# A GRU recurrence whose gate inputs are written to PSUM by ScalarE instead of matmuls

## The chip, the cores and the metric

The kernel runs on one core of a Trainium2 chip. Five engines work beside each other, each through its own instructions in order: TensorE (PE in the profile, its weight loads PEld), VectorE (DVE), ScalarE (ACT), GpSimd (POOL) and SyncE (SP), which here only issues DMA transfers. They wait for each other through semaphores. The metric is device time of one execution in microseconds (us), as the median of several runs; lower is better.

## What is computed

The reference adds four layers' outputs to x, of shape (4, 512, 512). The change lies in the third, a GRU over the 512 time steps of each of the 4 batch rows, with a state of 512:

```python
def cell(h, x):
    gi = x @ W_ih + b_ih
    gh = h @ W_hh + b_hh
    i_r, i_z, i_n = jnp.split(gi, 3, axis=-1)
    h_r, h_z, h_n = jnp.split(gh, 3, axis=-1)
    r = jax.nn.sigmoid(i_r + h_r)
    z = jax.nn.sigmoid(i_z + h_z)
    n = jnp.tanh(i_n + r * h_n)
    h_new = (1.0 - z) * n + z * h
    return (h_new, h_new)
xs = jnp.swapaxes(inputs, 0, 1)
_, hs = jax.lax.scan(cell, initial_state, xs)
...
x = x + _L0_cond_ref(...)          # top-k over masked attention
x = x + _L1_cond_ref(...)          # attention, 16 heads
x = x + _L2_cond_ref(cond_2048, x, L2_cond_W_ih, L2_cond_W_hh, L2_cond_b_ih, L2_cond_b_hh)   # the GRU
x = x + _L3_cond_ref(...)          # transformer block, called DiT below
```

The input products gi of all steps are made before the loop. What is left for the loop is h @ W_hh and the gates, one step after the other.

## The kernel before, in words

`program` runs the layers one after another: the top-k layer, the small attention, `gate_input_phase` (it computes gi of all 512 steps), `gru_phase` (the recurrence), `dit_phase`. Between two phases all engines meet at a barrier. The change lies in `gru_phase`.

**Layout.** A column vector of 512 lies as KD = 4 chunks of 128 partitions, with B = 4 batch columns each. Chunks 0 and 1 are the half called a (`first`), chunks 2 and 3 the half called b (`second`). W_hh is split in two fp16 parts, `w_hh_hi` and `w_hh_lo`; so is the state (`state_parts`). The product needs weights hi by both state parts (`high`, 8 moving columns) and weights lo by the high part of the state (`low`, 4 columns). A gate's half needs 2 output chunks by 4 contraction chunks. One `low` or `high` call is 4 matmuls, each with its own weight load; a step calls them 24 times, 96 matmuls in all. There are four PSUM banks for the r and z gates of the two halves (`sum_ra`, `sum_rb`, `sum_za`, `sum_zb`), of 16 columns in use each, and four for the n gate (`sum_n`: two parities of the step by two halves).

**Where gi enters.** For r and z, gi of all steps lies in the SBUF buffer `room` as two fp16 parts (`gi_rz`). SyncE copies it, two steps at a time, into `gi_now` (two buffers), and four matmuls per step (`bring`, L1494) multiply it with a scaled identity and so open the four gate banks with it. For n, ScalarE copies `gi_n` of the next step into a slot of the n bank (`copy_gi_n`, L1590); TensorE waits for it on the semaphore `gn_ready`.

**One step.** TensorE: four `bring` matmuls, each behind a wait for VectorE's reading of that bank; the wait for `hi_a`, the new high part of the state's half a; 12 calls up to the last one for ra (`ra_sum`); 8 more, which end za, na, rb and zb (`rb_sum`, `zb_sum`); 4 calls for the half b of n. VectorE sums a gate bank's two parts (`total`, L1650), scans (`chain`, L1654) for r * h_n + gi_n and for the new state, and makes the low part of the state. ScalarE makes the sigmoids and tanhs. The new half a of the state comes out as: `ra_sum`, total of ra, sigmoid (L1601), scan for n (L1654), tanh (L1607), scan for the state (L1654, `hi_a`). Half b follows the same way, up to `hi_b` and `lo_b`, which TensorE waits for later in the next step.

**Order.** It is written out by hand for every engine. ScalarE's in a step is r, z and keep of half a (L1601, L1603, L1604), `copy_gi_n` for the next step (L1590), tanh of a (L1607), r, z and keep of half b (L1609, L1611, L1612), tanh of b (L1614), and a copy of the new state to the history (L1617). TensorE loops over four steps, ScalarE and VectorE over two.

**After the loop.** SyncE loads the DiT layer's first weights into `region[1]` and `region[0]`, the two halves of `room`, once the last `gi_now` has been loaded from there; TensorE turns the history back, VectorE adds it to X, and SyncE stores three quarters of X to DRAM (`x_gru`). The phase ends when these stores have landed.

## Time and profile before

| | us |
|---|---|
| median of 3 runs | 4073.15 |
| lowest and highest | 4071.14, 4074.32 |
| span of the profiled execution | 4078.2 |
| first gate-input matmul of step 0 | 1079.5 |
| first gate-input matmul of step 511 | 2494.6 |

The profile is of one execution of its own, whose span, from the first to the last instruction, is 5.05 us (0.12%) over the median of the timed runs; no other time of that execution is given. Times in its rows are counted from the start of the span. Start and duration of an instruction stand in front of its engine and line; a row for several matmuls in a row has their count behind (x4) and their time from the first one's start to the last one's end. The end of a matmul is modelled, its start is recorded. Instructions on one engine overlap in part, so the start of one to the start of the next is what counts, not the duration.

### The profile page before, as it was taken

To read this page: it belongs to the slowest core of one execution; us is meant where nothing else is said; L and a number is where in the kernel's file an instruction comes from. 1 tells how busy PE (TensorE), PEld (TensorE's weight loads), DVE (VectorE), ACT (ScalarE), POOL (GpSimd) and SP (SyncE) were. 2 spreads that over 40 slices of the span, in tenths; PEclk is the share of its full clock that TensorE was granted. 3 is DMA by queue.
4 is the path that set the end of the run, shared out by engine and by line. 5 is a ranking of instruction groups with operands and counts; after the bars stand their busy time and mean duration, and the time that the engine had idled before them with its cause. 6 is when DMAs were issued, how large, how long until landed. Compare 5 with 4: busy or idle time off the path is not lost. (4 is left out here: it accounts for less than half of the span.)

```text
span 4078.2 us, 177223 instructions
## 1 busy us (share of the span) xinstructions
PE 3719.3 (91%) x70140; PEld 2792.5 (68%) x70140; DVE 2749.4 (67%) x10621; ACT 2082.2 (51%) x7371; POOL 478.1 (12%) x411
## 2 busy tenths in 40 slices
PE   2458888888999999999999998999999999999999
PEld 2425465554699999999999996565456546644664
DVE  8878788786677777777777776576367537653763
ACT  4028678677755555555555553453245315532542
POOL 2006366364000000000000000001000100010001
PEclk9979999998755555555555556999999999999999
DMA  2023132231000000000000003211221141023102
GB/s 93 1 89 94 48 110 87 60 106 56 4 6 6 6 6 6 6 6 6 6 6 6 6 6 137 83 41 42 109 90 34 42 158 52 23 83 124 44 14 93
DMA packets 113888, 203.31 MB, mean 50 GB/s; under 512 B 44076, under 2 KB 76844, under 8 KB 111416
## 3 DMA queue, kind: packets, MB, share of 16 engines
q1 hardware_dynamic: 113720, 201.00, 14.8%
q8 instruction: 114, 1.87, 0.2%
q14 instruction: 54, 0.44, 0.0%
HBM read 160.05 MB, written 32.52 MB: 47 GB/s over the span
## 5 line engine op out<-in xcount | busy, mean ns | idle before, releaser
L1521 PE MATMUL gru_sum_n<-gru_state_parts,w_hh_hi 128*128 128x8 f16 x8192 | 499.6, 174 | 0.0
L1511 PE MATMUL gru_sum_n<-gru_state_parts,w_hh_lo 128*128 128x4 f16 x8192 | 488.9, 168 | 0.0
L1511 PEld LDWEIGHTS gru_sum_n<-gru_state_parts,w_hh_lo 128*128 128x128 f16 x8192 | 376.5, 104 | 0.0
L1521 PEld LDWEIGHTS gru_sum_n<-gru_state_parts,w_hh_hi 128*128 128x128 f16 x8192 | 376.5, 104 | 0.0
L653 ACT ACTIVATE dit_prob<-dit_bank,dit_head_nbias 128x512 f32<-128x512 f32 x256 | 175.9, 687 | 351.0 <-DVE dit_head_nbias L671 350.6
L1654 DVE TENSOR_TENSOR_SCAN gru_n_in<-gru_reset_gate,gru_sum_n 128x32 f32<-128x32 f32 x1024 | 225.4, 220 | 54.7
L1511 PE MATMUL gru_sum_rb<-gru_state_parts,w_hh_lo 128*128 128x4 f16 x4096 | 261.3, 168 | 0.0
L1521 PE MATMUL gru_sum_za<-gru_state_parts,w_hh_hi 128*128 128x8 f16 x4096 | 254.1, 169 | 0.0
L1521 PE MATMUL gru_sum_ra<-gru_state_parts,w_hh_hi 128*128 128x8 f16 x4096 | 254.1, 168 | 0.0
L1521 PE MATMUL gru_sum_zb<-gru_state_parts,w_hh_hi 128*128 128x8 f16 x4096 | 254.1, 168 | 0.0
L1511 PE MATMUL gru_sum_zb<-gru_state_parts,w_hh_lo 128*128 128x4 f16 x4096 | 252.1, 166 | 0.0
L1511 PE MATMUL gru_sum_ra<-gru_state_parts,w_hh_lo 128*128 128x4 f16 x4096 | 252.1, 166 | 0.0
L1511 PE MATMUL gru_sum_za<-gru_state_parts,w_hh_lo 128*128 128x4 f16 x4096 | 252.1, 166 | 0.0
L1650 DVE TENSOR_REDUCE gru_r_in<-gru_sum_ra 128x8 f32<-128x16 f32 x512 | 89.2, 174 | 240.9 <-PE gru_sum_ra L1521 240.9
L1601 ACT ACTIVATE gru_reset_gate<-gru_r_in 128x8 f32<-128x8 f32 x512 | 111.1, 217 | 272.9 <-DVE gru_r_in L1650 272.9
L1654 DVE TENSOR_TENSOR_SCAN gru_state_parts<-gru_keep_gate,gru_new_and_old 128x24 f16<-128x24 f32 x1024 | 212.3, 207 | 45.8
L1617 ACT ACTIVATE gru_hist<-gru_state 128x16 f32 x512 | 118.7, 232 | 238.1 <-DVE gru_state L1654 238.1
L1844 POOL TENSOR_TENSOR dit_gated_bias<-dit_gates,dit_bias_rows 128x1024 f32<-128x1024 f32 x4 | 9.4, 2345 | 1835.8 <-DVE dit_bias_rows L2129 1559.8
L635 PE MATMUL small_bank<-ident,small_prob 128*128 128x128 f32 x1024 | 165.9, 285 | 56.6 <-DVE small_turned L762 39.4
L1762 PE MATMUL dit_bank<-dit_qk 128*128 128x512 f16 x768 | 207.6, 379 | 1.3 <-DVE dit_qk L2142 1.3
L539 PE MATMUL dit_bank<-room,dit_V 128*128 128x512 f16 x512 | 195.6, 382 | 10.3 <-DVE dit_V L2210 10.3
L756 ACT ACTIVATE small_prob<-small_bank,small_head_nmax 128x512 f32<-128x512 f32 x256 | 176.2, 690 | 54.3 <-DVE small_head_nmax L665 49.9
(335 smaller groups left out, 12378.5 us busy)
## 6 DMA issues: line engine op xcount, KB each, us to landing
dit_w_qk<-w_qk_parts SPq DMA_DIRECT2D x64, 512.0 KB, 3.6
room<-w_parts SPq DMA_DIRECT2D x8, 4096.0 KB, 12.8
room<-w_v_parts SPq DMA_DIRECT2D x5, 4096.0 KB, 12.2
room<-w_out_parts SPq DMA_DIRECT2D x4, 4096.0 KB, 14.8
small_given_w<-in_L_cond_qkv_w SPq DMA_DIRECT2D x48, 256.0 KB, 3.1
w_qk_parts<-small_parts_w SPq DMA_DIRECT2D x32, 256.0 KB, 2.1
small_given_w<-in_L_cond_ffn_w SPq DMA_DIRECT2D x32, 256.0 KB, 3.7
w_parts<-small_parts_w SPq DMA_DIRECT2D x32, 256.0 KB, 2.4
```

The costliest lines, as they stand in the source:

```text
L539: pe.matmul(out, lh, rh, start=start, stop=False)
L635: mm = pe.transpose(self.PT[t % 2][:, s * P:(s + 1) * P], self.prob[:, t % 2, s * P:(s + 1) * P], self.ident)
L653: act.activation(self.prob[:, t % 2, :], self.S[t % 2], ACT.Exp, bias=bias[:, t:t + 1], scale=self.scale, accum_out=self.rsum[:, t:t + 1]) ...
L756: act.activation(self.prob[:, t % 2, :], self.S[t % 2], ACT.Exp, bias=self.nmax[:, t:t + 1])\
L1511: mm = pe.matmul(columns[:, j, 0], w_hh[1][:, k, c:c + P], parts[:, par, 0, k, :, LAST], start=opens, stop=False, skip_group_check=True)
L1521: mm = pe.matmul(columns[:, j], w_hh[0][:, k, c:c + P], parts[:, par, :, k, :, LAST], start=opens, stop=False, skip_group_check=True)
L1601: act.activation(reset[:, A, :, GATED], r_in[:, A], ACT.Sigmoid, scale=1.0 / GS).then_inc(r_a, 1)
L1617: act.activation(hist[:, :, :, at(i)].rearrange("p f b o -> p f (b o)"), state[:, 1 - par, :, :, LAST], ACT.Copy).then_inc(kept, 1)
L1650: return dve.tensor_reduce(out, columns.rearrange("p (f e b) -> p f b e", e=2, b=B), AX.X, ALU.add)
L1654: return dve.tensor_tensor_scan(line(out), line(factor), line(term), 0.0, ALU.mult, ALU.add)
L1762: mm = pe.matmul(s, qk[:, hs.parity, 0, qe, t * P:(t + 1) * P], qk[:, hs.parity, 1, ke, :], start=(qe + ke == 0), stop=(qe == 1))
L1844: pool.tensor_tensor(gb[:], gates[:], rows[:], ALU.mult).then_inc(gated, 1)
```

## The change

- The four `bring` matmuls of a step, their identity, `gi_now` and its DMA copies go.
- ScalarE writes the gate inputs of the next step straight from `gi_rz` into the gate banks: `seed(i + 1, 0)` for the two banks of half a, between keep and tanh of half a, and `seed(i + 1, 1)` for those of half b, after keep of half b. Each is one ACTIVATE over 128 partitions by 2 banks by 16 columns. The four banks are allocated as one buffer, `sum_rz`, for this.
- `copy_gi_n(i + 1, ...)`, which stood between keep and tanh of half a, now stands behind `seed(i + 1, 1)`, between keep and tanh of half b.
- TensorE opens the four banks once, ahead of the loop, with a matmul of zeros, and always adds to what is there. At the top of each step it waits for `seeded_a`, `gn_ready` and `hi_a`, then begins with the `low` call for the half a of n; it waits for `seeded_b` ahead of the fourth call.
- SyncE issues the loads of the DiT weights once `seeded_b` stands at T = 512, the last seed.
- ScalarE's last two steps stand behind its loop, since the very last has nothing to seed.

```diff
@@ SyncE
-            for v in range(2):
-                sp.dma_start(gi_now[v][:], gi_rz[:, v * NOW:(v + 1) * NOW]).then_inc(now_loaded[v], 16)
-            with sp.Fori(0, T // (2 * NOW) - 1) as n:
-                for v in range(2):
-                    sp.wait_ge(now_taken[v], n + 1)
-                    sp.dma_start(gi_now[v][:], gi_rz[:, at(n * (2 * NOW) + (2 + v) * NOW, NOW)])\
-                      .then_inc(now_loaded[v], 16)
-            for v in range(2):
-                sp.wait_ge(now_loaded[v], 16 * (T // (2 * NOW)))
+            sp.wait_ge(seeded_b, T)
             sp.dma_start(region[1], store.out.rearrange("p e k n -> p e (k n)")).then_inc(first_loaded, 16)
             sp.dma_start(region[0], store.v.rearrange("p e k n -> p e (k n)")).then_inc(first_loaded, 16)
@@ TensorE
+            for bank in (ra_bank, za_bank, rb_bank, zb_bank):
+                mm = pe.matmul(bank[:, 0:HALF * 2 * B], const["ident16"][:], zero_columns[:], start=True, stop=False,
+                               skip_group_check=True)
+            mm.then_inc(banks_opened, 1)
...
-                    pe.wait_ge(z_in_a, i + 1)
-                    if o == 0:
-                        pe.wait_ge(now_loaded[v], n * 16 + 16)
-                    bring(za_bank, Z_GATE, first, v, o)
-                    pe.wait_ge(r_in_a, i + 1)
-                    bring(ra_bank, R_GATE, first, v, o)
-                    pe.wait_ge(r_in_b, i + 1)
-                    bring(rb_bank, R_GATE, second, v, o)
-                    pe.wait_ge(z_in_b, i + 1)
-                    mm = bring(zb_bank, Z_GATE, second, v, o)
-                    if o == NOW - 1:
-                        mm.then_inc(now_taken[v], 1)
+                    pe.wait_ge(seeded_a, i + 1)
+                    pe.wait_ge(gn_ready, i + 1)
                     pe.wait_ge(hi_a, i + 1)
-                    low(rb, R_GATE, second, first, par)
+                    low(na, N_GATE, first, first, par, opens=True)
                     low(za, Z_GATE, first, first, par)
                     low(ra, R_GATE, first, first, par)
+                    pe.wait_ge(seeded_b, i + 1)
+                    low(rb, R_GATE, second, first, par)
                     low(zb, Z_GATE, second, first, par)
-                    pe.wait_ge(gn_ready, i + 1)
-                    low(na, N_GATE, first, first, par, opens=True)
                     pe.wait_ge(lo_a, i + 1)
@@ ScalarE
+            def seed(i, half):
+
+                act.activation(gate_banks[:, half, :, 0:HALF * 2 * B],
+                               gi_rz[:, at(i), :, half * HALF:(half + 1) * HALF].rearrange("p o g k e b -> p (o g) (k e b)"),
+                               ACT.Copy, scale=GS / GIS).then_inc((seeded_a, seeded_b)[half], 1)
+
+            act.wait_ge(banks_opened, 1)
+            seed(0, 0)
+            seed(0, 1)
             copy_gi_n(0, 0)
```

On ScalarE, one step from the sigmoid of r of half a to the history, in the kernel before (`gru_reset_gate`, `gru_z_gate` and `gru_keep_gate` are the sigmoids of half a and then of half b, `gru_new_and_old` the tanhs; an ISA row sets an address register for the instruction behind it):

```order
L1601 ACTIVATE gru_reset_gate<-gru_r_in 128x8
L1603 ACTIVATE gru_z_gate<-gru_z_in 128x8
L1604 ACTIVATE gru_keep_gate<-gru_z_in 128x8
L1590 ISA
L1590 ACTIVATE gru_sum_n<-gi_n 128x2x8
L1607 ACTIVATE gru_new_and_old<-gru_n_in 128x8
L1609 ACTIVATE gru_reset_gate<-gru_r_in 128x8
L1611 ACTIVATE gru_z_gate<-gru_z_in 128x8
L1612 ACTIVATE gru_keep_gate<-gru_z_in 128x8
L1614 ACTIVATE gru_new_and_old<-gru_n_in 128x8
```

The same stretch of ScalarE's step in the changed kernel, from keep of half a on (L1574 is the seed, L1568 `copy_gi_n`):

```order
L1583 ACTIVATE gru_keep_gate<-gru_z_in 128x8
L1574 ISA
L1574 ACTIVATE gru_sum_rz<-room 128x2x16
L1587 ACTIVATE gru_new_and_old<-gru_n_in 128x8
L1589 ACTIVATE gru_reset_gate<-gru_r_in 128x8
L1591 ACTIVATE gru_z_gate<-gru_z_in 128x8
L1592 ACTIVATE gru_keep_gate<-gru_z_in 128x8
L1574 ISA
L1574 ACTIVATE gru_sum_rz<-room 128x2x16
L1568 ISA
L1568 ACTIVATE gru_sum_n<-gi_n 128x2x8
L1597 ACTIVATE gru_new_and_old<-gru_n_in 128x8
```

A seed took the place of the copy of gi_n in half a, and a second seed and the copy of gi_n stand behind the keep of half b.

On TensorE, the top of a step in the kernel before, after the last call of the step ahead of it:

```order
L1511 MATMUL gru_sum_n<-gru_state_parts,w_hh_lo 128x4 x4
L1533 REGISTER_ALU
L1494 MATMUL gru_sum_za<-gru_gi_now,gru_scaled_ident 128x16
L1494 MATMUL gru_sum_ra<-gru_gi_now,gru_scaled_ident 128x16
L1494 MATMUL gru_sum_rb<-gru_gi_now,gru_scaled_ident 128x16
L1494 MATMUL gru_sum_zb<-gru_gi_now,gru_scaled_ident 128x16
L1511 MATMUL gru_sum_rb<-gru_state_parts,w_hh_lo 128x4 x4
L1511 MATMUL gru_sum_za<-gru_state_parts,w_hh_lo 128x4 x4
```

The same place in the changed kernel, where the four gate banks go by one name, `gru_sum_rz` (the five `low` calls and the first `high` call):

```order
L1495 MATMUL gru_sum_n<-gru_state_parts,w_hh_lo 128x4 x4
L1521 REGISTER_ALU
L1495 MATMUL gru_sum_n<-gru_state_parts,w_hh_lo 128x4 x4
L1495 MATMUL gru_sum_rz<-gru_state_parts,w_hh_lo 128x4 x16
L1505 MATMUL gru_sum_rz<-gru_state_parts,w_hh_hi 128x8 x4
```

The four identity matmuls are gone, and the call that opens the n bank moved from the fifth place to the first.

## Rows read from the trace of the kernel before

**Rows 1.** The page's 40 slices: TensorE's busy tenths and granted clock.

```profile
PE   2458888888999999999999998999999999999999
...
PEclk9979999998755555555555556999999999999999
```

**Rows 2.** Windows: start:end, length, busy us (count) of PE, PEld, DVE, ACT, POOL, clock, DMA share, GB/s.

```profile
2000.00:2200.00 200.00, 199.80 (x7229) 198.29 (x7227) 146.36 (x1009) 116.22 (x721) 0.00 (x0) 0.50 0.03 6
```

**Rows 3.** The tile gru_sum_za: ns min/median/max, first and last start.

```profile
L1494 PE MATMUL gru_sum_za<-gru_gi_now,gru_scaled_ident x512: 173/173/193, 1079.5 to 2494.6; 128*128 128x16 f16 x171
```

**Rows 4.** Timeline of one step: start, duration, engine, line, operation.

```profile
1614.07 0.27 PE L1511 MATMUL gru_sum_rb<-gru_state_parts,w_hh_lo 128*128 128x4 f16 x4
...
1615.56 0.17 DVE L1650 TENSOR_REDUCE gru_r_in<-gru_sum_ra 128x8 f32<-128x16 f32 x1 [0.44 <-PE gru_sum_ra L1521]
...
1615.76 0.22 ACT L1601 ACTIVATE gru_reset_gate<-gru_r_in 128x8 f32<-128x8 f32 x1 [0.50 <-DVE gru_r_in L1650]
...
1616.05 0.22 DVE L1654 TENSOR_TENSOR_SCAN gru_n_in<-gru_reset_gate,gru_sum_n 128x32 f32<-128x32 f32 x1
1616.09 0.20 ACT L1604 ACTIVATE gru_keep_gate<-gru_z_in 128x8 f32<-128x8 f32 x1
1616.12 0.25 PE L1511 MATMUL gru_sum_zb<-gru_state_parts,w_hh_lo 128*128 128x4 f16 x4
1616.19 0.17 ACT L1590 ACTIVATE gru_sum_n<-gi_n 128x16 f32 x1
...
1616.30 0.22 ACT L1607 ACTIVATE gru_new_and_old<-gru_n_in 128x8 f32<-128x8 f32 x1
...
1616.41 0.17 DVE L1650 TENSOR_REDUCE gru_z_in<-gru_sum_zb 128x8 f32<-128x16 f32 x1
...
1616.55 0.21 DVE L1654 TENSOR_TENSOR_SCAN gru_state_parts<-gru_keep_gate,gru_new_and_old 128x24 f16<-128x24 f32 x1
1616.62 0.20 ACT L1611 ACTIVATE gru_z_gate<-gru_z_in 128x8 f32<-128x8 f32 x1
1616.66 0.17 PE L1494 MATMUL gru_sum_za<-gru_gi_now,gru_scaled_ident 128*128 128x16 f16 x1
...
1616.73 0.20 ACT L1612 ACTIVATE gru_keep_gate<-gru_z_in 128x8 f32<-128x8 f32 x1
1616.73 0.17 PE L1494 MATMUL gru_sum_zb<-gru_gi_now,gru_scaled_ident 128*128 128x16 f16 x1
1616.82 0.27 PE L1511 MATMUL gru_sum_rb<-gru_state_parts,w_hh_lo 128*128 128x4 f16 x4
...
1617.09 0.22 ACT L1614 ACTIVATE gru_new_and_old<-gru_n_in 128x8 f32<-128x8 f32 x1 [0.16 <-DVE gru_n_in L1654]
```

**Rows 5.** Timeline across the end of TensorE's loop over four steps.

```profile
1610.96 0.25 PE L1511 MATMUL gru_sum_n<-gru_state_parts,w_hh_lo 128*128 128x4 f16 x4
1610.97 0.21 DVE L1654 TENSOR_TENSOR_SCAN gru_state_parts<-gru_keep_gate,gru_new_and_old 128x24 f16<-128x24 f32 x1
...
1611.22 0.19 PE L1494 MATMUL gru_sum_za<-gru_gi_now,gru_scaled_ident 128*128 128x16 f16 x1
```

**Rows 6.** Groups of ScalarE between 1100 and 2480 us: count, busy us, mean ns.

```profile
L1617 ACT ACTIVATE gru_hist<-gru_state 128x16 f32 x499 | 115.7, 232 | 232.1 <-DVE gru_state L1654 232.1
```

**Rows 7.** Timeline from the last steps to the start of the DiT phase.

```profile
2485.66 0.35 SPq L1482 DMA_DIRECT2D room<-w_out_parts  x1
...
2494.72 0.27 PE L1511 MATMUL gru_sum_rb<-gru_state_parts,w_hh_lo 128*128 128x4 f16 x4
...
2498.40 0.23 ACT L1617 ACTIVATE gru_hist<-gru_state 128x16 f32 x1 [0.46 <-DVE gru_state L1654]
2498.69 1.11 PE L1581 MATMUL gru_sum_ra<-ident,gru_hist 128*128 128x128 f32 x4 [1.25 <-ACT gru_hist L1617]
...
2519.09 0.35 SPq L1783 DMA_DIRECT2D dit_qk_b<-in_qkv_b_columns  x1
```

**Rows 8.** Windows of that stretch, columns as in the second group.

```profile
2490.00:2495.00 5.00, 5.00 (x188) 5.00 (x185) 3.67 (x27) 3.01 (x20) 0.00 (x0) 0.50 1.02 439
...
2510.00:2515.00 5.00, 0.94 (x8) 0.52 (x5) 1.51 (x3) 0.00 (x0) 0.00 (x0) 1.00 1.05 408
2515.00:2519.00 4.00, 0.00 (x0) 0.00 (x0) 0.00 (x0) 0.00 (x0) 0.00 (x0) 0.54 0.13 49
```

77 lines of the change are left out of this document (38 added, 39 removed).

## The prediction

> **What bounds the kernel now.** The page's slices come first: in the recurrence TensorE reads 9 tenths and more busy while its granted clock stands at 5 tenths [rows 1], the lower of its two levels, 1.2 GHz. The window over 200 us says it closer: 199.80 us busy, clock 0.50 throughout [rows 2]. That looks like an engine that sets the pace, and like four matmuls less per step being a gain. So the next view is the timeline of one step, for what ends each wait [rows 4].
>
> The recurrence takes 2494.6 - 1079.5 = 1415.1 us for 511 steps, 2.769 us each [rows 3]. In the timeline a step goes from the first call of `low` at 1614.07 to that of the next step at 1616.82, 2.75 us [rows 4]. TensorE's own pitch: from 1614.07 to the call that ends zb at 1616.12 stand 19 calls, 76 matmuls, in 2.05 us, 27 ns each. A hundred matmuls make 2.70 us, and the missing 0.05 us stand at the top of the step: the last identity matmul starts at 1616.73, and the next one not 27 but 90 ns later. It waits for `hi_a`, whose scan starts at 1616.55 and takes 0.21: 1616.76, and TensorE starts 0.06 after that. The reader is to see a cycle through three engines: first call of the step, 48 matmuls to `ra_sum`, total at 1615.56, sigmoid at 1615.76, scan at 1616.05, tanh at 1616.30, scan of the state at 1616.55, first call of the next step. This cycle, 2.75 us long, sets the pace, and TensorE's queue is only 0.05 shorter than it. The four identity matmuls stand in the gap of this cycle.
>
> Once in four steps TensorE's loop turns. Its last call starts at 1610.96 and ends its issue 4 x 27 ns later, 1611.07; the first identity matmul starts at 1611.22 [rows 5], so that the first call follows at 1611.22 + 0.13 = 1611.35, when `hi_a` had been there since 1610.97 + 0.21 = 1611.18. Here the queue is the later one, by 0.11 us. Three steps of 2.745 and one of 2.85 make the mean of 2.77.
>
> **The change part by part.** Everything is counted from S, the start of a step's first call (S = 1614.07 in [rows 4]).
>
> *Removed: four identity matmuls, 4 x 27 ns = 0.11 us a step.* In three steps of four nothing is gained: without them TensorE stands at the wait for `hi_a` from 1616.66 on instead of 1616.76, and goes on at 1616.82 as before. At the turn of the loop up to 0.11 us would be gained, 128 x 0.11 = 14 us in all, if nothing else came late. Next point: something does. The DMA copies of `gi_now` load the engines by 3% [rows 2] and nobody waits for them: nothing.
>
> *Unchanged: the way from S to zb.* In the new order TensorE's calls up to `zb_sum` are again 20, of the same kinds; only the first five stand in another order. The total of zb starts at 1616.41, S + 2.34, and keep of half b on ScalarE at 1616.73, S + 2.66.
>
> *Moved: the copy of gi_n, and with it `gn_ready`.* This is the term that decides. Before, the copy was made at 1616.19, S + 2.12, behind keep of half a, and was done at S + 2.29, long before the call that needs it. Now it stands behind keep of half b and behind a seed, and TensorE asks for it at the very top of the next step, ahead of its first call. Queued behind that wait are all 24 calls of the step. The chain:
> - keep of half b starts at S + 2.66;
> - the seed of half b starts 0.10 later, as the copy does behind keep of half a now (1616.09 to 1616.19, with the same kind of address instruction in between): S + 2.76;
> - the copy of gi_n starts 0.10 after that, which I take for a seed because no pair of copies is in the trace, and the same pitch holds from keep to copy and (0.11) from copy to tanh: S + 2.86;
> - it takes 0.17 [rows 4]: S + 3.03;
> - TensorE starts 0.06 after its release, as after `hi_a`: S + 3.09.
>
> So the step grows to 3.09 us. Both `hi_a` (S + 2.69) and the turn of the loop (last call issued at about S + 2.6, and 0.15 for the turn) are earlier than that; the 0.11 at the turn is swallowed. Four steps take 12.36 in place of 4 x 2.769 = 11.08, so 1.28 x 128 = +164 us.
>
> *Added: two seeds a step.* That of half a stands where the copy stood. If it is as short as the copy, tanh of half a stays at S + 2.23; if longer, `hi_a` comes later, but `hi_a` has 0.34 us of room now. Its cover is that room. The one of half b is in the chain above. A seed's duration is not in the trace. It is a copy from SBUF to two PSUM banks, like L1590 (0.17), with 32 columns instead of 16; the longest small ACTIVATE of this phase is the history copy with 0.232 [rows 6], and if its successor did not overlap with it at all, the copy of gi_n would start 0.13 later. Bounds of a pitch: 0.07 and 0.23. I take 0.10, because L1590 is the nearest row in kind. Tanh of half b would be free to start at S + 2.97 and waits for its input until S + 3.02 (1617.09), as now.
>
> *Added: three waits on one matmul.* The trace shows no matmul that waits for three semaphores with the middle one last. Bounds: 0.03 less than the 0.06 of a single wait (ScalarE to VectorE takes about 0.03, tanh 1616.30 + 0.22 to 1616.55), and 0.06 more. I take 0.06 as for `hi_a`.
>
> The Trainium skill's page "ScalarE: Activation LUTs", in "What ACT_TABLE_LOAD costs", gives an ACTIVATE with immediate scale and bias 186 ns plus 0.833 ns a column, and lets neighbours overlap by 93 ns. The 16-column copy would be 199 ns by it, and the row has 170; the 32-column seed would be 213 ns with the next start 120 ns behind it, which is an estimate from that page and would make the step 0.02 us longer, 10 us more in all.
>
> *Before the loop:* opening the banks (4 matmuls), two seeds and the copy now stand ahead of the first call, about 0.1 + 0.17 + 0.06 + 2 x 0.10 + 0.17 + 0.06 = 0.8 us, where four identity matmuls took 0.13: +0.7 us, once.
>
> *After the loop:* the loads of the DiT weights were issued at 2485.66, 9.06 us before the first call of the last step at 2494.72 [rows 7]. Now they wait for the last `seeded_b`. That seed belongs to the step before the last and is done at S + 2.76 + 0.18, 0.15 us before the last step's S. So the loads start about 8.9 us later, seen from the last step. In the stretch behind them the DMA engines are full from 2490 on and again at 2510 to 2515, then empty [rows 8], and all other engines stand still until the DiT phase begins at 2519.09: the phase ends with its stores, and these share the engines with the loads. A later start moves the end by as much, less what the gaps between the stores give back. I take +8 us; bounds 5 and 9.
>
> Sum against the profile's own time: 4078.2 + 164 + 0.7 + 8 = 4251. The profile lies 5.05 us over the median, so 4073.15 + 173 = **4246 us**, 4.2% slower.
>
> **The rivals.**
>
> *A. `gn_ready` is not the late one.* For it speaks that the copy itself is short and ScalarE is idle for 0.16 us just before tanh of b [rows 4]. Against it: the copy is now behind keep of half b in the same queue, and that start, S + 2.66, is a row. If TensorE could start at `hi_a` all the same, the time would be 4073 - 14 + 0.7 + 8 = 4068, no change to speak of. 3%.
>
> *B. TensorE's own count decides (the faster side).* The reader of [rows 1, 2] would take 512 x 0.11 = 55 us off: 4073 - 55 + 9 = 4027. It needs the cycle through `hi_a` to be shorter than 2.70 us, and no late `gn_ready`. The 0.09 us ahead of the first call, where 27 ns are the pitch, speak against it. 2%.
>
> *C. The seeds cost more than a copy.* Without overlap and at the history copy's duration the copy of gi_n starts 0.13 later: 3.22 us a step, 67 us more, 4313; with 0.06 more for the triple wait 4343. For it: ScalarE's writes to two banks while TensorE writes others have no row at this size. Against it: L1590 writes two banks under the same conditions, 0.17 each time. 6% for over 4310.
>
> *D. TensorE's clock rises.* The gap at the top of a step would grow, and the clock was at 0.50 even with none [rows 2], so I see no reason for it. If the pitch of 27 ns were halved, the way from S to zb would lose 80 x 13.5 ns = 1.08 us a step: 4246 - 553 = 3693. 1%. The Trainium skill's page "TensorE: Matmul & The Clock Gate", Part 1, has sustained busy matmuls release the full clock; the window of 200 us at 99.9% busy and 0.50 does not agree for such narrow ones. By its section "Back-to-back issue gap" the pitch would not fall under about 25 ns in any case, an estimate of 80 x 2 ns = 0.16 us a step, or 82 us off.
>
> **How the numbers follow.** The forecast of a late `gn_ready` with prices within their bounds has 88%, A 3%, B 2%, C 6%, D 1%. Low end: pitches of 0.08 in place of 0.10 and a release of 0.03 make 3.02 us, 36 us less: 4210, rounded to 4212. High end: 3.21 us a step by a seed without overlap or by a dear triple wait, 4308, taken as 4310. What lies outside is A, B, D, the end of C and a few per cent besides. A measurement here tells about 0.2% (8 us) from no change. Faster by more: B and D, 3%. Within: A, 3%. Slower: 94%.
>
> **What would show it.** In the changed kernel's trace: a step of 3.09 us on average; the first call of a step 0.06 us behind the end of the copy of gi_n (L1568), and about 0.4 behind `hi_a`; TensorE's idle time ahead of L1495 released by ScalarE, about 0.4 us in each of 512 steps; keep of half b at S + 2.66; seeds of about 0.18. The loads of the DiT weights issued at the last step's S, and the DiT phase 8 us later from there. I am wrong if the first call starts with `hi_a`, if keep of half b stands elsewhere than S + 2.66, or if the clock in the recurrence is not 0.50.

## The result, and the profile after

| | before | after |
|---|---|---|
| median of 4 timed runs each, us | 4073.74 | 4266.03 |
| lowest and highest, us | 4071.14, 4074.61 | 4261.88, 4266.54 |
| span of the profiled execution, us | 4078.2 | 4264.8 |
| step, first to last history copy, by 511 | 2.769 | 3.116 |
| last history copy to the DiT layer's first VectorE result (`dit_bv_lo`), us | 27.4 | 36.1 |

After by before is 1.0468, with a 95% interval of 1.0453 to 1.0483: 4.7% slower. The forecast was 4246 us, 4.2%, with a range of 4212 to 4310, and the step was forecast at 3.09 us.

First the page of the changed kernel, its 40 slices (busy tenths and granted clock of TensorE), and from its costliest groups the one that begins a step (out<-in, shapes, count | busy us, mean ns of one | idle time of the engine just before, and what ended it):

```profile
PE   2468887879888888888888888799999999999999
...
PEclk9989999999555555555555555899999999999999
...
L1495 PE MATMUL gru_sum_n<-gru_state_parts,w_hh_lo 128*128 128x4 f16 x8192 | 489.2, 168 | 213.0 <-ACT gru_sum_n L1568 213.0
```

The nines of [rows 1] have become eights, and the clock is on the same level as before. The idle time ahead of a step's first call has a single releaser: ScalarE's copy of gi_n, L1568, 213.0 us over 512 steps, 0.42 us each. The next two rows say the same for parts of the recurrence: the waits between 1100 and 2600 us (engine, line waited for, us in total, times, longest), and the window that [rows 2] shows of before.

```profile
PE gru_sum_n L1495 <- ACT gru_sum_n L1568: 200.4, 482, 0.4
```

```profile
2000.00:2200.00 200.00, 173.14 (x6155) 169.31 (x6152) 130.46 (x901) 114.02 (x774) 0.00 (x0) 0.50 0.00 0
```

TensorE was busy for 199.80 of 200 us and is for 173.14 now; the clock is 0.50 in both. Nothing became slower on it, it waits. Where the wait comes from stands in the timeline of one step, to be laid beside [rows 4]. This step's first call started at S = 1614.23.

```profile
1616.23 0.20 ACT L1583 ACTIVATE gru_keep_gate<-gru_z_in 128x8 f32<-128x8 f32 x1
...
1616.33 0.18 ACT L1574 ACTIVATE gru_sum_rz<-room 128x32 f32 x1
...
1616.44 0.21 ACT L1587 ACTIVATE gru_new_and_old<-gru_n_in 128x8 f32<-128x8 f32 x1
...
1616.69 0.21 DVE L1644 TENSOR_TENSOR_SCAN gru_state_parts<-gru_keep_gate,gru_new_and_old 128x24 f16<-128x24 f32 x1
...
1616.86 0.20 ACT L1592 ACTIVATE gru_keep_gate<-gru_z_in 128x8 f32<-128x8 f32 x1
1616.96 0.18 ACT L1574 ACTIVATE gru_sum_rz<-room 128x32 f32 x1
...
1617.08 0.17 ACT L1568 ACTIVATE gru_sum_n<-gi_n 128x16 f32 x1
...
1617.35 0.25 PE L1495 MATMUL gru_sum_n<-gru_state_parts,w_hh_lo 128*128 128x4 f16 x4 [0.41 <-ACT gru_sum_n L1568]
```

The chain of the prediction stands there link by link: keep of half b, seed of half b, copy of gi_n, first call of the next step. The new state (`hi_a`) was finished at 1616.69 + 0.21 = 1616.90 and waited 0.45 us for a copy of data that had been known since before the recurrence began.

Over all steps the two new kinds of instruction on ScalarE (L1574 seed, L1568 copy; groups between 1100 and 2600 us, mean ns of one):

```profile
L1574 ACT ACTIVATE gru_sum_rz<-room 128x32 f32 x962 | 175.2, 182 | 0.0
...
L1568 ACT ACTIVATE gru_sum_n<-gi_n 128x16 f32 x481 | 79.4, 165 | 0.0
```

A seed of twice the columns takes 17 ns longer than the copy.

Last, the end of the phase, beside [rows 7, 8]: SyncE's queue, and windows of the stretch (columns as in [rows 2]).

```profile
2667.48 0.33 SPq L1472 DMA_DIRECT2D room<-w_out_parts  x1
2667.85 0.43 SPq L1473 DMA_DIRECT2D room<-w_v_parts  x1
2676.16 6.43 SPq L1477 DMA_DIRECT2D x_gru<-X  x3
2700.92 0.35 SPq L1773 DMA_DIRECT2D dit_qk_b<-in_qkv_b_columns  x1
```

```profile
2667.00:2672.00 5.00, 3.41 (x108) 3.27 (x105) 3.21 (x23) 2.57 (x16) 0.00 (x0) 0.50 0.84 315
...
2687.00:2692.00 5.00, 0.00 (x0) 0.00 (x0) 0.00 (x0) 0.00 (x0) 0.00 (x0) 0.51 0.89 290
2692.00:2697.00 5.00, 0.00 (x0) 0.00 (x0) 0.00 (x0) 0.00 (x0) 0.00 (x0) 0.50 1.05 410
```

The loads are issued at the last step's first call (2667.66), as forecast. From 2687 on only the DMA engines work, for ten microseconds; in before there was one window of five in which they were full and TensorE nearly idle [rows 8].

### The profile page after: what moved, and what is told of

It reads as the page before. It is cut to its first block and busy times, and to the rows that moved or that the text cites. A ratio compares the mean times of both kernels' runs of the same rounds, so it can differ in the third digit from the quotient of the medians.

```text
span 4264.8 us, 174784 instructions
## 1 busy us (share of the span) xinstructions
PE 3685.6 (86%) x68096; PEld 2737.9 (64%) x68096; DVE 2748.8 (64%) x10620; ACT 2164.3 (51%) x8394; POOL 479.5 (11%) x411
## 5 line engine op out<-in xcount | busy, mean ns | idle before, releaser
L1505 PE MATMUL gru_sum_rz<-gru_state_parts,w_hh_hi 128*128 128x8 f16 x16384 | 800.9, 169 | 0.0
L1495 PE MATMUL gru_sum_rz<-gru_state_parts,w_hh_lo 128*128 128x4 f16 x16384 | 777.3, 166 | 0.0
L1505 PEld LDWEIGHTS gru_sum_rz<-gru_state_parts,w_hh_hi 128*128 128x128 f16 x16384 | 674.3, 104 | 0.0
L1495 PE MATMUL gru_sum_n<-gru_state_parts,w_hh_lo 128*128 128x4 f16 x8192 | 489.2, 168 | 213.0 <-ACT gru_sum_n L1568 213.0
L1495 PEld LDWEIGHTS gru_sum_rz<-gru_state_parts,w_hh_lo 128*128 128x128 f16 x16384 | 634.7, 104 | 0.0
L1640 DVE TENSOR_REDUCE gru_r_in<-gru_sum_rz 128x8 f32<-128x16 f32 x1024 | 177.3, 173 | 419.2 <-PE gru_sum_rz L1505 419.2
L539 PE MATMUL dit_bank<-room,dit_V 128*128 128x512 f16 x512 | 197.2, 385 | 10.3 <-DVE dit_V L2200 10.3
L539 PE MATMUL dit_bank<-dit_yh,dit_w_qk 128*128 128x512 f16 x512 | 194.2, 379 | 8.8 <-DVE dit_V L2127 6.8
L541 PE MATMUL dit_bank<-room,dit_V 128*128 128x512 f16 x512 | 196.8, 384 | 0.0
L540 PE MATMUL dit_bank<-room,dit_V 128*128 128x512 f16 x512 | 196.6, 384 | 0.0
```

Source lines behind the costliest of these rows:

```text
L539: pe.matmul(out, lh, rh, start=start, stop=False)
L540: pe.matmul(out, lh, rl, start=False, stop=False)
L541: return pe.matmul(out, ll, rh, start=False, stop=stop)
L1495: mm = pe.matmul(columns[:, j, 0], w_hh[1][:, k, c:c + P], parts[:, par, 0, k, :, LAST], start=opens, stop=False, skip_group_check=True)
L1505: mm = pe.matmul(columns[:, j], w_hh[0][:, k, c:c + P], parts[:, par, :, k, :, LAST], start=opens, stop=False, skip_group_check=True)
L1640: return dve.tensor_reduce(out, columns.rearrange("p (f e b) -> p f b e", e=2, b=B), AX.X, ALU.add)
```

## The experiments

Twelve kernels, measured in three groups; each group has its own runs of before, with medians 4076.72 us (the first four below `after`), 4076.03 (the next four) and 4074.98 (the last four). "Step" is always the span from the first to the last history copy by 511, and "tail" the time from there to `dit_bv_lo`, both from the one profile that each kernel has.

| kernel | median us | ratio to before, 95% interval | step us | tail us |
|---|---|---|---|---|
| before | 4073.74 | | 2.769 | 27.4 |
| after | 4266.03 | 1.0468 (1.0453 to 1.0483) | 3.116 | 36.1 |
| copy_behind_tanh | 4112.57 | 1.0082 (1.0067 to 1.0098) | 2.813 | 36.8 |
| wait_fifth | 4109.11 | 1.0077 (1.0061 to 1.0092) | 2.814 | 36.2 |
| copy_before_tanh | 4156.64 | 1.0194 (1.0178 to 1.0209) | 2.908 | 36.1 |
| late_loads | 4085.51 | 1.0022 (1.0013 to 1.0031) | 2.770 | 37.7 |
| before_late_copy | 4179.83 | 1.0252 (1.0236 to 1.0268) | 2.978 | 23.8 |
| before_three_waits | 4101.40 | 1.0072 (1.0057 to 1.0087) | 2.820 | 27.0 |
| no_identity_one_wait | 4064.10 | 0.9977 (0.9967 to 0.9986) | 2.746 | 27.9 |
| one_wait | 4090.51 | 1.0036 (1.0022 to 1.0050) | 2.780 | 36.9 |
| spread_waits | 4076.22 | 1.0003 (0.9994 to 1.0012) | 2.744 | 36.7 |
| one_wait_split | 4081.83 | 1.0012 (1.0003 to 1.0021) | 2.780 | 25.3 |
| before_split | 4070.42 | 0.9988 (0.9979 to 0.9997) | 2.770 | 22.4 |
| spread_waits_split | 4064.30 | 0.9970 (0.9959 to 0.9981) | 2.745 | 25.9 |

The theory at the start was that of the prediction, a copy of gi_n that comes late to a wait at the top of the step. Its rivals: that the seeds themselves or their number cost the time, that the identity matmuls were worth much more than they seem, and that the waits have a price of their own.

### The place of the copy

`copy_behind_tanh` leaves everything of the change and moves one line: the copy of gi_n stands behind tanh of half a instead of behind the seed of half b.

```diff
@@ ScalarE
                 act.activation(mix[:, A, :, 0], n_in[:, A, :, GATED], ACT.Tanh, scale=1.0 / GS).then_inc(n_a, 1)
+                if more:
+                    copy_gi_n(i + 1, 1 - par)
...
                 if more:
                     seed(i + 1, 1)
-                    copy_gi_n(i + 1, 1 - par)
```

> The changed kernel with one ScalarE instruction moved: the copy of gi_n for the next step stands directly behind the tanh of half a, ahead of the sigmoid of r of half b, and no longer behind the second seed. Everything else as in the changed kernel, TensorE's waits at the top of the step too. My theory (the late copy of gi_n holds the first call of every step): the copy is done about 0.4 us before the new state's half a, TensorE is released by VectorE again, the step is 2.745 us with the turn of the loop hidden, so 511 steps take 1403 us in place of 1415 before and 1593 changed; with 9 us more behind the loop and 1 ahead of it 4072 us. Rival (the seeds themselves, as work on ScalarE or as writes to PSUM banks, are dear): the step stays over 3.0 us and the time over 4200. Rival (TensorE's count of matmuls decides): 96 x 27 ns = 2.6 us a step, about 4000 us.

Of the 0.347 us that the change had put on a step, this takes 0.303 away; the kernel takes 153 us less than the changed one, of the 192 that the change had added. The expected 2.745 us and 4072 were missed all the same, by 0.068 us a step and 41 us; what is left is the subject of "Three waits on one call".

### The place of the wait

`wait_fifth` leaves the copy where the change put it, and moves the call that needs it back to the fifth place of the step, with its wait.

```diff
@@ TensorE
                     pe.wait_ge(seeded_a, i + 1)
-                    pe.wait_ge(gn_ready, i + 1)
                     pe.wait_ge(hi_a, i + 1)
-                    low(na, N_GATE, first, first, par, opens=True)
                     low(za, Z_GATE, first, first, par)
...
                     low(zb, Z_GATE, second, first, par)
+                    pe.wait_ge(gn_ready, i + 1)
+                    low(na, N_GATE, first, first, par, opens=True)
                     pe.wait_ge(lo_a, i + 1)
```

> The changed kernel with TensorE's order undone and ScalarE's kept: the call that opens the n bank, and the wait for the copy of gi_n, stand fifth in the step again, behind the low calls of za, ra, rb and zb. The copy stays behind the second seed. My theory: in the changed kernel's trace the copy ends at S + 3.02, and the fifth call of a step of 2.745 us falls at S + 2.745 + 0.43 = S + 3.18, so the copy is just in time and the step is 2.745 us, 4072 us in all; where its release takes 0.10 us the room is 0.06 us. Rival (the seeds are dear in themselves): over 4200. If the room is too small by some hundredths, the step is 2.8 and the time about 4100.

The step is 2.814 us, to a thousandth what `copy_behind_tanh` has. So neither the copy's late place alone costs much nor the early wait alone; it takes both, and undoing either is worth the same. The expected 2.745 us were missed by the same 0.07 as above, and not for want of room ahead of the fifth call: the copy was done 0.20 us behind the first call, and the fifth starts 0.43 behind it.

### The copy ahead of tanh of half a

```diff
@@ ScalarE
                     seed(i + 1, 0)
+                    copy_gi_n(i + 1, 1 - par)
...
                     seed(i + 1, 1)
-                    copy_gi_n(i + 1, 1 - par)
```

> The changed kernel with the copy of gi_n back in half a, between the first seed and the tanh of half a. TensorE as in the changed kernel. My theory: the copy is early enough, but two instructions of about 0.11 us each stand between keep and tanh of half a where one stood, and there the cycle through the new state has no room: tanh of a starts about 0.10 us later, the step is 2.85 us, 4073.7 + 511 x 0.08 + 9.5 = 4124 us. Rival (ScalarE has room everywhere because it reads half busy): 4072, as with the copy behind the tanh.

2.908 us, 0.095 more than behind tanh of half a; the expected 2.85 had left out the price of three waits, like the two before it. Here the copy delays the tanh from which `hi_a` follows, by one pitch. On ScalarE an instruction of 0.17 us costs nothing where the engine has room and its whole pitch, here 0.10, on the cycle through `hi_a`.

### The move without the seeds

`before_late_copy` is the kernel before, identity matmuls and all, with only the copy and its wait moved. If the seeds are innocent of the rest, it must show the step of the chain less one seed.

```diff
@@ TensorE
+                    pe.wait_ge(gn_ready, i + 1)
                     pe.wait_ge(hi_a, i + 1)
+                    low(na, N_GATE, first, first, par, opens=True)
                     low(rb, R_GATE, second, first, par)
...
-                    pe.wait_ge(gn_ready, i + 1)
-                    low(na, N_GATE, first, first, par, opens=True)
@@ ScalarE
-                    copy_gi_n(i + 1, 1 - par)
                     act.wait_ge(n_in_a, i + 1)
...
                     act.activation(keep[:, Z, :, LAST], z_in[:, Z], ACT.Sigmoid, scale=-1.0 / GS).then_inc(keep_b, 1)
+                    copy_gi_n(i + 1, 1 - par)
```

> The kernel before, identity matmuls and all, with only the copy of gi_n moved behind keep of half b and with its wait and its call at the top of a step. No seeds. My theory (the position of the copy is what costs): copy at S + 2.66 + 0.10 = 2.76, done at 2.93, first call at 3.03 us: 0.26 us a step more than before, 133 us, 4210. Rival (seeds are what costs): as before, 4076.

The step is 2.978 us, above before's 2.769 and below the 3.03 expected, which had taken 0.10 for the release. The timeline of this kernel, a step whose first call started at S = 1612.70 (L1590 is the copy, L1511 the first call):

```profile
1612.70 0.24 PE L1511 MATMUL gru_sum_n<-gru_state_parts,w_hh_lo 128*128 128x4 f16 x3
...
1615.36 0.20 ACT L1611 ACTIVATE gru_keep_gate<-gru_z_in 128x8 f32<-128x8 f32 x1
...
1615.45 0.17 ACT L1590 ACTIVATE gru_sum_n<-gi_n 128x16 f32 x1
...
1615.68 0.27 PE L1511 MATMUL gru_sum_n<-gru_state_parts,w_hh_lo 128*128 128x4 f16 x4
```

Keep of half b at S + 2.66, the copy 0.09 behind it, done at S + 2.92, the first call at S + 2.98. This is the prediction's chain without the seed, with its own prices: 2.66, a pitch, 0.17 and 0.06. In the changed kernel the seed adds its pitch of 0.12, and the release is 0.10 instead of 0.06; 2.978 + 0.12 + 0.04 less the 0.03 by which keep of half b stands earlier there is 3.11. So the move makes 0.21 of the 0.347 us. The other 0.14 came with the seed and with the third wait, its semaphore `seeded_a`, all of it on the same chain.

### What the identity matmuls had cost

`no_identity_one_wait` is the kernel before without the four identity matmuls and without the copies into `gi_now`; the first call of a bank opens it. It leaves out the gate inputs of r and z, so its time is that of a step in which they enter for nothing. Its DiT loads, which have no last `gi_now` to wait for any more, wait for the history of step T - 5.

```diff
@@ TensorE
-                    pe.wait_ge(z_in_a, i + 1)
-                    if o == 0:
-                        pe.wait_ge(now_loaded[v], n * 16 + 16)
-                    bring(za_bank, Z_GATE, first, v, o)
-                    pe.wait_ge(r_in_a, i + 1)
-                    bring(ra_bank, R_GATE, first, v, o)
-                    pe.wait_ge(r_in_b, i + 1)
-                    bring(rb_bank, R_GATE, second, v, o)
-                    pe.wait_ge(z_in_b, i + 1)
-                    mm = bring(zb_bank, Z_GATE, second, v, o)
...
                     pe.wait_ge(hi_a, i + 1)
-                    low(rb, R_GATE, second, first, par)
+                    low(rb, R_GATE, second, first, par, opens=True)
```

> The kernel before without its four identity matmuls and without the DMA copies that feed them; the first call into each gate bank opens it, so the gate inputs of r and z are left out of what is computed. The only wait ahead of a step's first call is the one for the new state's half a. It shows what taking the four matmuls away is worth by itself. My theory (the cycle through hi_a sets the pace): nothing in three steps of four, 0.11 us at the turn of the loop, 14 us in all: 4062 against 4076. Rival (TensorE's count): 55 us less, 4021. In the two kernels with the copy of gi_n made early the first call started 0.14 us behind hi_a and not 0.06. Of that there are two readings: a TensorE that stands idle at the wait starts later than one that arrives just then; then this kernel's step is 2.81 us and it takes 4098 us. Or a call held by two or three semaphores starts later than one held by one; then this kernel stays at 4062.

It gains 12 us, 0.024 us a step, not 55. All that these 2048 matmuls had cost on the path was the queue's delay at the turn of TensorE's loop, which the prediction had put at 14 us: in before the first call comes 0.17 us behind `hi_a` in one step of four and 0.06 in the others, here 0.06 in all. That bounds what any way of bringing in the gate inputs of r and z could have gained in the loop.

### Three waits on one call

Both `copy_behind_tanh` and `wait_fifth` stay 0.044 us a step above before, although `hi_a` is again the last to come. In `wait_fifth` the scan of `hi_a` ends at 1614.33 + 0.21 = 1614.54 and the first call starts at 1614.69, 0.15 later, where before has 0.06. `before_three_waits` asks whether waits that were fulfilled long before cost anything: before, with two such waits more on the step's first call.

```diff
@@ TensorE
+                    pe.wait_ge(r_in_a, i + 1)
+                    pe.wait_ge(gn_ready, i + 1)
                     pe.wait_ge(hi_a, i + 1)
                     low(rb, R_GATE, second, first, par)
```

> The kernel before, with two waits more on a step's first call, for the total of ra and for the copy of gi_n, both fulfilled long before hi_a. Nothing else. If the number of semaphores on the call costs the time: the first call starts 0.14 us behind hi_a in place of 0.06 in each step that waits for it, up to 0.08 x 512 = 41 us more, about 4110. If it is TensorE's idle queue that costs: no change, 4076.

They cost 25 us, 0.050 a step (expected were up to 41 us). Its timeline, the scan that makes `hi_a` and the step's first call (L1511), the identity matmuls in between:

```profile
1617.14 0.21 DVE L1656 TENSOR_TENSOR_SCAN gru_state_parts<-gru_keep_gate,gru_new_and_old 128x24 f16<-128x24 f32 x1
...
1617.32 0.17 PE L1494 MATMUL gru_sum_zb<-gru_gi_now,gru_scaled_ident 128*128 128x16 f16 x1
...
1617.50 0.25 PE L1511 MATMUL gru_sum_rb<-gru_state_parts,w_hh_lo 128*128 128x4 f16 x4
```

From the scan's end, 1617.35, to the call are 0.15 us; in [rows 4] it is 0.06. A step gets 0.07 of these 0.09: in before the first matmul of the call stands 0.048 us ahead of the second, in this kernel and in `wait_fifth` 0.025. And it gets them in three steps of four only, since at the turn of the loop TensorE is later than `hi_a` anyway; that makes the 0.050. Another reading had been that not the number of waits but an idle queue ahead of them makes TensorE start late. `no_identity_one_wait` speaks against it: there the queue is empty ahead of the single wait, and the call starts 0.05 behind the scan's end.

```profile
1616.58 0.21 DVE L1634 TENSOR_TENSOR_SCAN gru_state_parts<-gru_keep_gate,gru_new_and_old 128x24 f16<-128x24 f32 x1
...
1616.84 0.27 PE L1503 MATMUL gru_sum_rb<-gru_state_parts,w_hh_lo 128*128 128x4 f16 x4
```

The traces show what the further waits are. A call with more than one of them has an instruction of its own ahead of its first weight load, EVENT_SEMAPHORE, which does nothing but wait. Here it is in `wait_fifth` (two waits), in `before_late_copy` (two) and in the changed kernel (three), with its shortest, middle and longest duration in ns and its first and last start; the kernels with one wait have none on that call.

```profile
L1522 PEldq EVENT_SEMAPHORE  x512: 51/51/51, 1079.6 to 2517.8; - x171
...
L1546 PEldq EVENT_SEMAPHORE  x512: 51/51/51, 1076.6 to 2598.1; - x171
...
L1523 PEldq EVENT_SEMAPHORE  x512: 347/355/644, 1074.3 to 2667.2; - x171
```

The semaphores recorded with it are those of the later `wait_ge` lines; the one written first is recorded with the weight load behind it. In `wait_fifth` `hi_a` is the second line. So EVENT_SEMAPHORE starts 0.04 us behind the scan's end, at 1614.58, and takes 0.05; the weight load follows at 1614.66 and the matmul at 1614.69. In `before_late_copy` the instruction has `hi_a` too, but is over at 1615.48, and the late one, `gn_ready`, is on the weight load: the matmul starts 0.06 behind the copy's end, as with a single wait. So by these traces it is not the number of waits that costs the 0.09 us, but that the last to come sits on the extra instruction.

### One wait at the top

`one_wait` is the changed kernel with its seeds, the copy behind tanh of half a, and only `hi_a` on the first call. `seeded_a` needs no wait inside the loop: tanh of half a follows it in ScalarE's queue, so that `hi_a` implies it.

```diff
@@ TensorE
+            pe.wait_ge(seeded_a, 1)
             with pe.Fori(0, T // TURN) as n:
...
-                    pe.wait_ge(seeded_a, i + 1)
-                    pe.wait_ge(gn_ready, i + 1)
                     pe.wait_ge(hi_a, i + 1)
-                    low(na, N_GATE, first, first, par, opens=True)
                     low(za, Z_GATE, first, first, par)
                     low(ra, R_GATE, first, first, par)
                     pe.wait_ge(seeded_b, i + 1)
                     low(rb, R_GATE, second, first, par)
                     low(zb, Z_GATE, second, first, par)
+                    pe.wait_ge(gn_ready, i + 1)
+                    low(na, N_GATE, first, first, par, opens=True)
```

> The changed kernel with the copy of gi_n behind the tanh of half a, with the call that opens the n bank fifth in the step behind its own wait, and with the wait for seeded_a taken out of the loop (one stands ahead of it): hi_a, which ScalarE's tanh of half a precedes, implies it. So a step's first call is held by one semaphore. If the number of semaphores costs: a step of 2.745 us, with the turn of the loop hidden, and 9 us more behind the loop: 4076 - 12 + 9 + 1 = 4074. If the idle queue costs: 2.81 us as in the kernel with the copy behind the tanh, 4110.

The step falls to 2.780, but not to the 2.746 of `no_identity_one_wait`. The timeline shows why (L1574 is the seed of half b; the row of 16 matmuls is the first four calls, the next one is the fifth):

```profile
1614.09 0.21 DVE L1645 TENSOR_TENSOR_SCAN gru_state_parts<-gru_keep_gate,gru_new_and_old 128x24 f16<-128x24 f32 x1
...
1614.35 0.62 PE L1495 MATMUL gru_sum_rz<-gru_state_parts,w_hh_lo 128*128 128x4 f16 x16
1614.36 0.18 ACT L1574 ACTIVATE gru_sum_rz<-room 128x32 f32 x1
...
1614.83 0.25 PE L1495 MATMUL gru_sum_n<-gru_state_parts,w_hh_lo 128*128 128x4 f16 x4
```

The release from `hi_a` is 0.05 again (1614.30 to 1614.35). But the fifth call starts 0.48 behind the first, in `no_identity_one_wait` 0.45 (1614.10 to 1614.55). The seed of half b ends at 1614.54, and the third call, which waits for it, was due at 1614.35 + 0.24 = 1614.59, by the 0.24 us that it stands behind the first call in `no_identity_one_wait`. It starts at 1614.60, 0.06 behind the seed's end, which is 0.01 late; and since it had to be released, its second matmul follows after 0.05 us instead of 0.03. Together that is 0.03 us. `spread_waits` puts the n call third and gives the seed time until 1614.35 + 12 x 0.027 = 1614.67.

```diff
@@ TensorE, against one_wait
                     low(ra, R_GATE, first, first, par)
+                    pe.wait_ge(gn_ready, i + 1)
+                    low(na, N_GATE, first, first, par, opens=True)
                     pe.wait_ge(seeded_b, i + 1)
                     low(rb, R_GATE, second, first, par)
                     low(zb, Z_GATE, second, first, par)
-                    pe.wait_ge(gn_ready, i + 1)
-                    low(na, N_GATE, first, first, par, opens=True)
```

> As one_wait, but TensorE's low call for the half a of n, with its wait for gn_ready, stands third, and the wait for seeded_b with the calls for rb and zb stands behind it: each wait on a call of its own, and seeded_b is asked for 0.32 us behind the first call instead of 0.22. In one_wait's trace the fifth call started 0.46 us behind the first where 16 matmuls of 27 ns make 0.43, and seed b ended 0.19 us behind the first call. Theory (a late seeded_b costs one_wait 0.03 us a step): the fifth call starts at 0.43 and the step falls from 2.780 to about 2.75, 15 us less, 4075 us, no change against before (the tail still costs 9 us and the loop gives 10). Rival (the 0.03 us are a price of the added waits themselves or of the seed ahead of tanh of a, wherever they stand): the step stays at 2.78 and the time at 4090.

The step is 2.744 us, that of the kernel without any gate inputs: all seeds are hidden. In its timeline (rows of 8, 4 and 8 matmuls, then the sixth call) the sixth call starts 0.56 behind the first; in `one_wait` that was 0.59.

```profile
1613.97 0.38 PE L1495 MATMUL gru_sum_rz<-gru_state_parts,w_hh_lo 128*128 128x4 f16 x8
1613.98 0.18 ACT L1574 ACTIVATE gru_sum_rz<-room 128x32 f32 x1
...
1614.21 0.25 PE L1495 MATMUL gru_sum_n<-gru_state_parts,w_hh_lo 128*128 128x4 f16 x4
...
1614.31 0.35 PE L1495 MATMUL gru_sum_rz<-gru_state_parts,w_hh_lo 128*128 128x4 f16 x8
...
1614.53 0.22 PE L1505 MATMUL gru_sum_rz<-gru_state_parts,w_hh_hi 128*128 128x8 f16 x3
```

The kernel as a whole is level with before, 1.0003, since the loop's gain, 511 x 0.025 = 13 us, goes into the tail, 9.3 us longer, and the DiT part, 4.1 us longer in this pair of profiles.

### The loads behind the loop

`late_loads` delays the loads of the DiT weights in the kernel before to the last step and changes nothing else.

```diff
@@ SyncE
                 sp.wait_ge(now_loaded[v], 16 * (T // (2 * NOW)))
+            sp.wait_ge(kept, T - 1)
             sp.dma_start(region[1], store.out.rearrange("p e k n -> p e (k n)")).then_inc(first_loaded, 16)
```

> The kernel before with one wait more on SyncE: the loads of the DiT weights behind the loop also wait until ScalarE has kept step 510's history, which is about 1 us after the last step's first call. The recurrence is as before. My theory (the end of the phase is bound by the transfers' throughput, and so moves with their start): the loads start 10 us later, and the DiT phase starts 8 to 10 us later: 4083 us. Rival (the stores of X end last whenever the loads begin, the loads are hidden): 4074, no difference.

8.8 us in the time and 10.3 in the tail, for loads that are issued 10.4 us nearer to the last history copy (2489.02 and 2491.4 here, 2485.66 and 2498.4 in before). So the transfers set the end of the phase, and the prediction's price for the late loads stands by an experiment of its own.

The cut of the loads follows from this: once step 256 has been seeded, the first half of `room` is free, and with it one of the two destinations.

```diff
@@ SyncE, against spread_waits and one_wait
+            sp.wait_ge(seeded_b, T // 2)
+            sp.dma_start(region[0], store.v.rearrange("p e k n -> p e (k n)")).then_inc(first_loaded, 16)
             sp.wait_ge(seeded_b, T)
             sp.dma_start(region[1], store.out.rearrange("p e k n -> p e (k n)")).then_inc(first_loaded, 16)
-            sp.dma_start(region[0], store.v.rearrange("p e k n -> p e (k n)")).then_inc(first_loaded, 16)
```

In `before_split` SyncE's loop over the copies into `gi_now` is cut in two at step 256, with the load of `region[0]` between the halves:

```diff
@@ SyncE, against before
-            with sp.Fori(0, T // (2 * NOW) - 1) as n:
+            with sp.Fori(0, T // (4 * NOW) - 1) as n:
...
+            for v in range(2):
+                sp.wait_ge(now_loaded[v], 16 * (T // (4 * NOW)))
+            sp.dma_start(region[0], store.v.rearrange("p e k n -> p e (k n)")).then_inc(first_loaded, 16)
+            with sp.Fori(0, T // (4 * NOW)) as n:
+                for v in range(2):
+                    sp.wait_ge(now_taken[v], n + T // (4 * NOW))
...
-            sp.dma_start(region[0], store.v.rearrange("p e k n -> p e (k n)")).then_inc(first_loaded, 16)
```

> As spread_waits, with the loads of the DiT weights cut apart: the half of room that holds the gate inputs of steps 0 to 255 is loaded anew at step 256, and only the other at the last seed. Half of the traffic leaves the phase's end. Theory (transfers bound the end of the phase): the tail, 36.9 us in one_wait, falls to 25 us (between 23 and 27.4), which takes 12 us off spread_waits: 4063 us, 0.3% faster than before. Rival (the end is bound by the chain of transposes, additions and stores): the tail stays over 33 us and the time is 4072 or more.

> one_wait with the same cut of the loads. Theory: the step stays 2.780 and the tail falls to 25 us, so 4090.5 - 12 = 4078 us. The difference to spread_waits_split is then the price of the late seeded_b alone, 15 us. Rival: the tail is bound otherwise, 4087 or more.

> The kernel before, with its identity matmuls and DMA copies, and the same cut of the loads: one half of room is loaded anew at step 256, the other where both were. It tells how much of a faster version is owed to the cut and not to the seeds. In before the end of the phase had both loads 9 us ahead of the last step, and the DMA engines were full up to 2505 and again at 2510 to 2515. Theory: the stores no longer share the engines with the loads, and the tail falls from 27.4 to about 25 us, so 4073 us. If the loads 9 us ahead hinder nobody: no change, 4076.

The tail falls from 36.7 to 25.9 us in the one and from 36.9 to 25.3 in the other. `spread_waits_split` takes 4064.30 us, 0.30% less than before (0.19 to 0.41%): it is faster than both kernels of this case. Against `one_wait_split`, from the same call, it saves 17.5 us, where 0.035 x 511 = 18 are due to the late seed of half b. `before_split` shows what of this is owed to the cut alone: 4.6 us, with a tail of 22.4, shorter than expected. The changed kernel's idea, done well, is worth 6 us more than that, 4070.42 to 4064.30; the slowest of the 8 runs of the one, 4066.59, is below the fastest of the 11 of the other, 4067.41. In the queue of `spread_waits_split` the second load goes out 0.2 us behind the last step's first call, 2481.03, and the DiT phase begins 22.7 us behind that call; in the changed kernel that was 33.3.

```profile
2481.25 0.32 SPq L1474 DMA_DIRECT2D room<-w_out_parts  x1
2489.54 6.17 SPq L1478 DMA_DIRECT2D x_gru<-X  x3
2503.73 0.35 SPq L1775 DMA_DIRECT2D dit_qk_b<-in_qkv_b_columns  x1
```

## Why the prediction was right, and where its sizes were off

**The bound.** Right. The cycle through `hi_a` and not TensorE's count set the step of before: without the identity matmuls it is 2.746 (forecast 2.745), and rival B's 55 us are 12 in `no_identity_one_wait`.

**The moved copy.** Right in mechanism, and shown from both sides: undoing the copy's place, or the wait's, takes 0.303 us of 0.347 away, and doing the move alone puts 0.21 on. Its price was mis-sized, 0.32 us forecast on a mean step and 0.347 measured, 177 us in place of 164. By its links, counted from S:

| link | forecast | after |
|---|---|---|
| keep of half b starts | 2.66 | 2.63 |
| keep to seed | 0.10 | 0.10 |
| seed to copy | 0.10 | 0.12 |
| the copy | 0.17 | 0.17 |
| its end to the first call | 0.06 | 0.10 |
| step | 3.09 | 3.12 |

The term that was mis-sized by most is the release: I took the 0.06 of a single wait where bounds of 0.03 and 0.12 had stood beside it, and `gn_ready` sits on EVENT_SEMAPHORE here, with `hi_a`. The pitch behind a seed is 0.02 longer than behind a copy. Keep of half b is 0.03 earlier, against a forecast that nothing would move there: behind three waits the first matmul of a step stands 0.025 us ahead of the second, in before 0.048, so all that follows stands 0.02 nearer to S. Two terms were taken too small and one too large; that they cancel in part is luck.

The prediction had cited the Trainium skill's page "ScalarE: Activation LUTs", section "What ACT_TABLE_LOAD costs", for an estimate of 120 ns from the seed's start to the next; the trace agrees (1616.96 to 1617.08). By the same section of the Trainium skill the durations would be 213 and 199 ns, and the rows have 182 and 165. So its two terms are both off for a seed, since 182 less 120 leaves an overlap of about 60 ns and not its 93, and only their difference is right.

**The identity matmuls.** Right: nothing gained in the changed kernel, and 12 us (forecast up to 14) where no new wait takes their place.

**The seed of half a.** Right that its room covers it. `hi_a` ends at S + 2.67 and has 0.45 us until the first call. The seed starts 0.10 behind keep of half a, as the copy did, and tanh of half a 0.11 behind the seed.

**Three waits on a call.** Taken at the price of one. `before_three_waits` shows that this is wrong in general: 0.15 instead of 0.06. In the changed kernel the awaited one stood in the middle, and the release took 0.10: EVENT_SEMAPHORE, which had begun with `hi_a`, ended 0.04 behind the copy, and the matmul started 0.06 behind that.

**Ahead of the loop.** Forecast +0.7 us. From the opening of the banks at 1074.14 to the first call at 1075.04 are 0.90 us, 0.77 over the 0.13 of the identity matmuls.

```profile
1074.14 0.28 PE L1513 MATMUL gru_sum_rz<-gru_gru_zeros,ident 128*128 128x16 f16 x4 [6.07 <-DVEq L1636]
1074.52 0.32 ACT L1574 ACTIVATE gru_sum_rz<-room 128x32 f32<-128x32 f16 x2 [3.25 <-PE gru_sum_rz L1513]
1074.77 0.17 ACT L1568 ACTIVATE gru_sum_n<-gi_n 128x16 f32<-128x16 f32 x1
...
1075.04 0.22 PE L1495 MATMUL gru_sum_n<-gru_state_parts,w_hh_lo 128*128 128x4 f16 x3 [0.62 <-ACT gru_sum_n L1568]
```

**The tail.** Forecast +8, measured +8.7, and `late_loads` gives 8.8 us for the delay by itself.

**The sum.** The spans differ by 186.6 us: 177.4 in the loop, 8.7 in the tail, 5.1 more in the DiT layer, 4.6 less ahead of the first history copy. The last two are no part of the prediction. Ahead of the recurrence the profiles of all these kernels scatter by 7.7 us, from 1076.0 to 1083.7 for the first history copy, and before's was among the long ones. That would explain why the medians differ by more, 192.3, than the spans. The DiT part lies between 1552.2 and 1558.0 us in the fourteen profiles. It is 1554.2 to 1558.0 in all kernels with both loads at the end, but 1554.9 in `before_late_copy` and 1555.0 in `one_wait_split` as well, which load both or one of them early. What lengthens it stays open: no run was made for it, each kernel has one profile, and windows over its first 300 us show the same work in the same time.

Against the forecast's 173 us the medians show 192: 13 of the missing 19 are the step's and 1 is the tail's; for the other 5 I have only the longer DiT part to name.

**The rivals.** A (`gn_ready` is not late) is refuted by the releaser of 512 waits. B by the experiment above. C asked for a pitch of 0.23 and got 0.12. D: the clock is 0.50 in the loop, though TensorE now idles for an eighth of it.

## What to carry to other kernels

When a change puts a buffer's refill on another engine, write down for each refill where it stands in that engine's queue and which call of the consumer asks for it first, both from the timeline; here 0.35 us a step hung on the two together, and undoing either took most of it away. A busy share of 99.9% does not say that an engine sets the pace: the 0.09 us ahead of the first call, where 0.027 are the pitch, said that it did not, and taking work from it gave a fifth of its time back. Put the semaphore that comes last on a call that waits for nothing else, and spread the others over later calls, each with its own. Where a call must have two, the rows here speak for writing the late one first; no pair of kernels that differ in this order alone was run.

## What the hardware showed that I had not expected

**Waits that are fulfilled still delay a release.** From the end of the scan that makes `hi_a` to the first matmul: 0.05 to 0.06 us with one wait on the call ([rows 4], `no_identity_one_wait`, `one_wait`); 0.15 with two (`wait_fifth`, a scan at 1614.33 + 0.21 and a call at 1614.69) and with three (`before_three_waits`, `copy_before_tanh`, `copy_behind_tanh`), though all the others had been fulfilled long before. The awaited semaphore was the last one written in all of these. Where it was another, the release was shorter: 0.10 as the second of three in the changed kernel, 0.06 as the first of two in `before_late_copy`. The trace gives the place as the reason: all waits but the first written are on an EVENT_SEMAPHORE ahead of the weight load. The awaited semaphore was always VectorE's in the slow cases and ScalarE's in these two; that this is not the reason is seen from the single waits, 0.06 for either (`hi_a` in before, `seeded_b` in `one_wait`).

**An idle queue costs nothing.** TensorE started 0.05 behind its release with nothing in the queue ahead of the wait (`no_identity_one_wait`), and 0.06 with the identity matmuls there ([rows 4]).

**ScalarE fills PSUM beside TensorE's writes at its usual speed.** The seeds took 180 to 201 ns in 1024 cases of the changed kernel. In the loop those of half a took 181 or 182 ns, while TensorE started seven matmuls into other banks; those of half b 180 to 183, while it stood waiting.
